# Another prologue order, score copies by ScalarE, and output turns in score slots, in an attention stage of a fused kernel

## The reference, cut to what matters

```
q, k = rope(x @ Wq, x @ Wk);  v = x @ Wv;  beta = x @ Wb + bb
p = softmax over j < i of (k_i . k_j) / 4          # strictly lower
A = p * beta + identity                             # lower triangular
u = solve_triangular(A, v)
o = softmax over j <= i of (q_i . k_j) / 4  applied to u;  out = o @ Wo
```

## Time and profile before

| | |
|---|---|
| time, median of 3 runs | 1138.64 us (1136.46 to 1138.84) |
| the profiled execution's own time | 1140.44 us |
| its span (first to last instruction) | 1138.5 us |
| busy: TensorE, weight loads | 742.7 us, 528.0 us |
| busy: VectorE, ScalarE, GpSimd | 562.3 us, 299.1 us, 238.5 us |
| mean granted TensorE clock | 0.799 |
| last instruction of the attention block | 505.98 us |
| inversions start (line 677) | 116.65, 207.61, 302.70, 395.14 us |

### The profile page before, as it was taken

One profiled execution on the slowest core, in us unless ns is written; L12 is line 12 of the kernel. 1 busy time (PEld: TensorE's weight loads), 2 busy tenths in 40 slices (PEclk: granted clock), 3 DMA queues, 4 the chain that ended last, 5 costly groups with the idle time before them and its releaser, 6 DMA issues. The chain is left out here.

```text
span 1138.5 us, 16783 instructions
## 1 busy us (share of the span) xinstructions
PE 742.7 (65%) x6078; PEld 528.0 (46%) x6079; DVE 562.3 (49%) x1556; ACT 299.1 (26%) x494; POOL 238.5 (21%) x251
## 2 busy tenths in 40 slices
PE   1967387777767757762054999998004550999980
PEld 1533264355445436442043999997001240566650
DVE  6796985885788582136300333333346551233322
ACT  1005144442542543311021344443002210211110
POOL 8003002111120210001775000004576005000005
PEclk9897689878979965666576999999556765899995
DMA  3691005122340901017934888886232002111113
GB/s 121 98 138 44 0 3 176 29 32 46 133 57 7 397 12 39 1 49 242 392 130 158 302 297 293 291 291 226 66 100 88 1 0 81 36 43 45 46 37 111
DMA packets 71264, 132.53 MB, mean 116 GB/s; under 512 B 11424, under 2 KB 35360, under 8 KB 70176
## 3 DMA queue, kind: packets, MB, share of 16 engines
q1 hardware_dynamic: 59168, 96.92, 28.9%
q0 software_dynamic: 7680, 20.98, 5.7%
q10 hardware_dynamic: 4352, 13.77, 3.2%
HBM read 77.18 MB, written 54.26 MB: 115 GB/s over the span
## 5 line engine op out<-in xcount | busy, mean ns | idle before, releaser
L1096 PE MATMUL scores<-wgu,zero 128*128 128x192 f32 x512 | 101.7, 345 | 2.7 <-DMA wd<-in_wd 2.7
L806 ACT ACTIVATE E<-scores 128x1280 f32<-128x1280 f32 x64 | 77.0, 1237 | 85.2 <-PE scores L354 54.0
L613 DVE TENSOR_REDUCE block_maxima<-scores 128x10 f32<-128x1280 f32 x64 | 92.3, 1486 | 12.5 <-PE scores L338 11.6
L1197 DVE TENSOR_TENSOR val<-sel,scores 128x192 f32<-128x192 f32 x64 | 22.7, 354 | 149.5 <-ACT sel L1239 149.5
L1253 POOL DMA_INDIRECT expert_rows<-xn_moe,scatter_slots x64 | 62.6, 977 | 133.2 <-DVE gather_slots L1173 114.0
L1096 PEld LDWEIGHTS scores<-wgu,zero 128*128 128x128 f32 x512 | 88.9, 204 | 3.2 <-DMA wd<-in_wd 3.1
L1580 PE MATMUL scores<-w,xgT 128*128 x184 | 88.8, 607 | 0.5 <-issue 0.5
L1089 PE MATMUL misc<-cf,xg 128*128 128x128 f32 x256 | 42.2, 290 | 65.2 <-DMA xg<-expert_rows 65.2
L1230 ACT COPY zero<-misc 128x512 f32<-128x512 f32 x64 | 37.5, 586 | 136.2 <-PE misc L1089 136.2
L911 POOL TENSOR_SCALAR_AFFINE_SELECT E<-E 128x256 f32<-128x256 f32 x64 | 27.0, 447 | 219.4 <-ACT E L806 219.3
L1113 PE MATMUL scores<-wd,slot 96*128 96x256 f32 x256 | 68.2, 391 | 0.5 <-ACT slot L1226 0.5
(11 more groups left out here) (232 smaller groups left out, 1526.1 us busy)
## 6 DMA issues: line engine op xcount, KB each, us to landing
expert_rows<-zero SPq DMA_DIRECT2D x32, 512.0 KB, 6.2
xg<-expert_rows SPq DMA_DIRECT2D x64, 256.0 KB, 3.4
expert_outputs<-xnT SPq DMA_DIRECT2D x64, 256.0 KB, 2.9
wgu<-in_wgu SPq DMA_DIRECT2D x32, 384.0 KB, 3.6
w<-in_w ACTq DMA_DIRECT2D x8, 1024.0 KB, 16.5
wd<-in_wd SPq DMA_DIRECT2D x32, 192.0 KB, 3.8
w<-in_w ACTq DMA_DIRECT2D x8, 512.0 KB, 19.0
split_heads<-E SPq DMA_DIRECT2D x8, 384.0 KB, 4.6
```

The lines of the kernel that those rows point to most:

```text
L613: nc.vector.tensor_reduce(bm[:, c, h, :], scores[:, slot, 0:WIDE].rearrange("p (a n) -> p a n", n=P), AX.X, ALU.max).then_inc(s_fd, 1)
L806: nc.scalar.activation(Eu(u)[:, h, :], scores[:, k % 2, 0:WIDE], ACT.Exp, scale=SCALE).then_inc(s_fa, 1)
L1096: ins = nc.tensor.matmul(scores[:, j % 2, t * 2 * F0:(t + 1) * 2 * F0], xgT[:, j % 2, k, t * P:(t + 1) * P], wgu[:, j // GE, j % GE, k, :] ...
```

## The change

What it does, part by part:

- **First rows.** The clears of the upper rows of unit 0's stacks go from GpSimd to VectorE's start. The rows of ones are filled as float pairs (`TWO_ONES`) over half as many elements. The clears of XT and XR both come after the normalization.
- **Heads by index first.** The columns of Wq and Wk are ordered so that a partition is dimension * 8 + head. A stack slot is then one contiguous piece of DRAM, 16 rows of 8 KB. The B stack is loaded in three copies (48, 32 and 16 rows) instead of six. ScalarE's queue issues the first k stack.
- **Projections 4 to 7** are made after row scores 3, 6, 9 and 12. ScalarE copies each into SBUF (`held`), and VectorE rotates them after the maxima of unit 0. Projection 3 and the beta columns change places.
- **First maxima.** The k maxima of unit 0 are turned before row score 10, and key score 0 comes before the turn of the q maxima.
- **Gather.** It collects in `turned` and no longer in `Y`; VectorE takes 12 of 16 copies instead of 8. Y's identity blocks are written in the prologue and in the solve of the unit before.
- **Sums** wait for the first transpose (`LB`) only, `join` for the second. The outputs of unit u-1 are divided after T1 steps 0 and 1 of unit u.
- **Output turns** go to the score slots 0 and 1, both after `attend(u, 1)`; the second half's copy goes to `bankD`.
- **Last unit.** Its q scores are made between the steps of its solve (`beside`), their exponentials go to the other half of E (`Eq`). Wo is loaded into `LB` after the last sums, not into E.

```diff
-PART_A = (0, 0, 1, 1, 0, 2)
-PART_B = (0, 1, 0, 1, 2, 0)
+RUNS_A = tuple((s, p, 1) for s, p in enumerate((0, 0, 0, 1, 1, 2)))
+RUNS_B = ((0, 0, 3), (3, 0, 2), (5, 0, 1))
...
+            def Eq(u):
+
+                return EE[:, u % 2] if u + 1 < UNITS else EE[:, (u + 1) % 2]
...
             def load_stack(q, u, c):
-                hg, b = unit(u)
-                x, order = {"k": (0, PART_A), "B": (0, PART_B), "q": (1, PART_A)}[c]
-                for s, part in enumerate(order):
-                    q.dma_start(stk[c][HD * s:HD * (s + 1), u % 2],
-                                scr[x, part, hg * P:(hg + 1) * P, b * T:(b + 1) * T]
-                                .rearrange("(h d) n -> d h n", d=HD)).then_inc((s_stq if c == "q" else s_stk)[u % 2], 16)
+                done = (s_stq if c == "q" else s_stk)[u % 2]
+                for s, part, n in RUNS_B if c == "B" else RUNS_A:
+                    to = stk[c][HD * s:HD * (s + n), u % 2].rearrange("p h n -> p (h n)")
+                    of = scr[int(c == "q"), u, part:part + n].rearrange("t (d h) n -> (t d) (h n)", h=GH)
+                    q.dma_start(to, of).then_inc(done, 16)
...
+            held = {4: EE[:, 0, 5, 0:2 * T], 5: EE[:, 0, 7, 0:2 * T], 6: AO_flat[:, 0:2 * T], 7: AO_flat[:, 2 * T:4 * T]}
...
-                    for w in range(5):
+                    for w in range(3):
                         project(w)
-                    pe.wait_ge(s_rf, 3)
+                    pe.wait_ge(s_rf, 1)
...
                     ins.then_inc(s_v, 1)
+                    project(3)
                     pe.wait_ge(s_vc, 1)
-                    project(5)
-                    pe.wait_ge(s_rf, 5)
-                    pe.wait_ge(s_ones, 1)
+                    pe.wait_ge(s_ones, 2)
...
+                    def beside(u, heads):
+
+                        if u + 1 < UNITS:
+                            key_scores(u + 1, heads)
+                        else:
+                            pe.wait_ge(s_ml[1], 48 * (u + 1))
+                            for h in heads:
+                                transposed_scores(u, 1, h)
...
                     def turn_outputs(u, hh):
                         pe.wait_ge(s_oc, 2 * u + hh + 1)
+                        pe.wait_ge(s_fa, use(1, u) + GH)
+                        of = bankD if hh else bankT
                         for it in range(NI):
-                            ins = nc.tensor.transpose(misc[:, hh, it * P:(it + 1) * P], bankT[:, it * P:(it + 1) * P], identf)
+                            ins = nc.tensor.transpose(scores[:, hh, it * P:(it + 1) * P], of[:, it * P:(it + 1) * P], identf)
...
+                        if m == 10:
+                            turn_maxima(0, 0)
+                            pe.wait_ge(s_mr, 1)
                         row_scores(0, m, m % 2)
-                    turn_maxima(0, 0)
+                        if m in (3, 6, 9, 12):
+                            project(m // 3 + 3)
+                    key_scores(0, [0])
                     turn_maxima(0, 1)
                     pe.wait_ge(s_mr, 2)
-                    key_scores(0, [0, 1])
-                    project(6)
-                    key_scores(0, [2, 3, 4])
-                    project(7)
-                    key_scores(0, [5, 6, 7])
+                    key_scores(0, range(1, GH))
...
-                        pe.wait_ge(s_y, 2 * (u + 1))
-                        if u:
-                            pe.wait_ge(s_fa, use(1, u - 1) + GH)
-                            pe.wait_ge(s_ao, 2 * u)
-                        else:
+                        pe.wait_ge(s_y, 2 * u + 1)
+                        if u == 0:
                             pe.wait_ge(s_vc, 1 + NT)
...
+                    for c in ("B", "k", "q"):
+                        ins = nc.vector.memset(upper_rows(c, 0), 0.0)
+                    ins.then_inc(s_z0, 1)
...
-                        for s in range(2, P // SB):
+                        for s in range(1, P // SB):
...
-                        link(nc.vector.transpose(LB[:].rearrange("p j i -> p i j"), Y[:]))
-                        link(nc.vector.memset(Y[:], 0.0))
-                        nc.vector.memset(flat[:, 0:SB * SB - 1].rearrange("p (a b) -> p a b", b=SB + 1)[:, :, 0], 1.0)
-                        link(nc.vector.memset(flat[:, SB * SB - 1:SB * SB], 1.0))
+                        link(nc.vector.transpose(LB[:].rearrange("p j i -> p i j"), turned[:]))
...
                     for m in range(16):
                         maxima(0, m, m % 2)
...
-                    for w in range(5, 8):
+                    for w in range(4, 8):
                         rotate_and_split(w)
...
                             scaled_sums(u, q)
+                            if u and q < 2:
+                                outputs(u - 1, q)
...
+                    act.wait_ge(s_pw[0], 16)
+                    load_stack(act, 0, "k")
...
+                    def hold(w):
+                        act.wait_ge(s_pj, w + 1)
+                        nc.scalar.copy(held[w], misc[:].rearrange("p b n -> p (b n)")).then_inc(s_rf, 1)
+
+                    hold(4)
+                    hold(5)
                     rows(0, 0)
+                    hold(6)
+                    hold(7)
                     rows(0, 1)
...
+                    for c in ("B", "k", "q"):
+                        zero_rows(c, 1)
+                    one_rows(1)
+                    pool.wait_ge(s_z0, 1)
+                    one_rows(0)
                     link(nc.gpsimd.memset(zero[:], 0.0))
                     nc.gpsimd.sem_inc(s_ones, 1)
-                    link(nc.gpsimd.memset(XT[:], 0.0))
-                    nc.gpsimd.sem_inc(s_z, 1)
                     pool.wait_ge(s_xn, NT)
                     link(nc.gpsimd.memset(XR, 0.0))
+                    nc.gpsimd.sem_inc(s_z, 1)
+                    link(nc.gpsimd.memset(XT[:], 0.0))
                     nc.gpsimd.sem_inc(s_z, 1)
...
                     sp.wait_ge(s_pw[0], 16)
-                    load_stack(sp, 0, "k")
+                    load_stack(sp, 0, "B")
                     store_parts(sp, 1)
-                    load_stack(sp, 0, "B")
```

More of the change, by code:

```diff
@@ L323, in turn_maxima @@
                         pe.wait_ge(s_nms, 2 * u + c + 1)
-                        pe.wait_ge(s_fd, 16 * u + (9 if u and not c else 16))
+                        pe.wait_ge(s_fd, 16 * u + (16 if c else 9))
                         nc.tensor.transpose(scores[0:96, c, WIDE:WIDE + 64].bitcast(BF16),
@@ L445, in solve @@
                                 ins.then_inc(s_s, 1)
-                                if not last:
-                                    key_scores(u + 1, [2 * it + 1])
+                                beside(u, [2 * it + 1])
                                 pe.wait_ge(s_sn, 3 * u + it)
@@ L460, in solve @@
                             ins.then_inc(s_us, 1)
-                            if not last:
-                                if it < NI - 1:
-                                    key_scores(u + 1, [2 * it + 2] if it else [0, 1, 2])
-                                else:
-                                    denominators(u + 1)
+                            if it < NI - 1:
+                                beside(u, [2 * it + 2] if it else [0, 1, 2])
+                            elif not last:
+                                denominators(u + 1)
                             pe.wait_ge(s_un, 4 * u + it + 1)
@@ L538, in _ @@
                                 for m in maxima_due(q):
+                                    if u and m < 2:
+                                        pe.wait_ge(s_ao, 2 * u - 1 + m)
                                     if m >= 2:
@@ L549, in _ @@
                         solve(u)
+                        if last:
+                            pe.wait_ge(s_uv, 4 * (u + 1))
+                            attend(u, 0)
+                            attend(u, 1)
+                            turn_outputs(u, 0)
+                            turn_outputs(u, 1)
+                            break
                         pe.wait_ge(s_ml[1], 48 * (u + 1))
                         transposed_scores(u, 1, 0)
-                        if not last:
-                            turn_denominators(u + 1)
-                            turn_g(u + 1)
-                            pe.wait_ge(s_g, u + 2)
+                        turn_denominators(u + 1)
+                        turn_g(u + 1)
+                        pe.wait_ge(s_g, u + 2)
                         pe.wait_ge(s_uv, 4 * (u + 1))
@@ L602, in rotate_and_split @@
                         nc.vector.sem_inc(s_parts, 1)
-                    for w in range(5):
+                    identity_blocks()
+                    for w in range(4):
                         rotate_and_split(w)
-                    dve.wait_ge(s_vc, 1)
-                    bcol = VB[:, :, D:D + H]
-                    link(nc.vector.tensor_tensor(bcol, bcol, bb[:].unsqueeze(1).to_broadcast([P, NT, H]), ALU.add))
```

(11 more changed lines are left out.)

112 lines of the change are left out of this document (63 added, 49 removed).

## The result

The changed kernel took 1106.83 us, the median of 4 runs (1105.47 to 1107.94), against 1138.74 for the kernel before, measured beside it: a ratio of 0.9721, 95% interval 0.9700 to 0.9742. The profiled execution took 1105.99, span 1104.1, mean granted clock 0.811. Forecast was 1103.5.

A forecast was written before the change was run, and what follows sets the result against it. The first block was taken as a sequence of stages, read by each stage's last wait. Gains 8.0 + 4.2 + 8.1 + 16.2 = 36.5 from 1140.4 gave 1103.9, stated as 1103.5; range 1093 to 1119.

The forecast's parts named there:

- Prologue: Start to first inversion: its first multiplication comes at 108.7 instead of 116.65, gain 8.0, bounds −2 and 12.5.
- the rotations would have lost 7: Rotations 4 to 7 beside GpSimd's selects: 0.5 charged, bounds 0 and 7; the skill's two-SBUF-input rule would make it 7.
- Stacks: Prologue: k and B stack loads land at 45.6, before VectorE arrives at 46.0; at 109 GB/s 48.7, costing 2.7.
- Rival 3: Stack copies get worse, contiguous sources reaching few engines; whole gain eaten, or time near 1187; chance 0.03.
- Between units: Three times, gather to inversion 1.4 each, 4.2; earlier T1 and later output divisions in units 1 to 3, 8.1.
- Last unit: q scores between the solve's steps, at the clock of unit 0: last division at 475.4 against 491.61, gain 16.2.
- Rival 1: The last solve stays at 1.2 GHz: 14 less gain, 1118; chance 0.15.
- My first paragraph: Change touches only the first of four blocks, ending near 506; what is saved there moves everything behind one for one.
- some 2: Last step of the sum: 1103.9 is some 2 less if measured as the median was; forecast stated as 1103.5.

The follow-up runs named there:

- e4: Changed kernel with the last unit's eight q scores and exponentials behind the solve again; ratio 0.9756 to the kernel before, on the slower chip.
- e5: e4 with the same score matmuls also issued between the solve's steps, read by nobody; 1110.91 us against 1140.27 for the kernel before, ratio 0.9741.
- e7: Changed kernel with nine filler float matmuls, read by nobody, at the start of blocks 2 and 4; 1107.10 us, ratio 0.9723 to the kernel before.
- e1: Changed kernel with GpSimd's clears in the old order and number, XT cleared before the normalization; ratio 0.9772 to the kernel before.
- e2: Changed kernel with the gather split 8 and 8 again and identity blocks set behind its transpose; block ended 7.5 us later than the changed kernel's, no total given.
- e3: Changed kernel with the first sums waiting for both transposes of an inversion; block ended 6.7 us later than the changed kernel's, no total given.
- e9: Changed kernel with five filler float matmuls, read by nobody, at the start of blocks 2 and 4; 1101.33 us, ratio 0.9672 to the kernel before.

## Why the prediction was right

- **Prologue: 8.0 forecast, 9.2 measured.** The normalization ended at 15.8 (15.2 forecast): the three VectorE clears end at 7.8, behind X's arrival, and cost 1.4, not 0.2. The first projection started at 18.51 (18.0), the first rotation at 22.32 (23.6). This last gain is luck as far as these runs show: with the same code up to there the rotation started at 22.3 in four profiles and at 24.1 to 24.5 in three (e4, e5, e7), where the multiplication came at 108.5 to 109.4. Projection 3 took 6.44 at the low clock (6.1). The maxima ran from 44.76 to 80.06 (46.0 to 81.85) with stalls of 2.60, 2.50, 1.49 and 2.49 (four of 2.5). The four rotations behind them took 19.4 and not 18.6, 0.8 more (0.5). The inversion started at 107.49 (108.7).
- **GpSimd against VectorE.** With GpSimd idle all eight instructions took 0.41, and e1 brought 3.75 back. The Trainium skill (SBUF — State Buffer, "Who interferes with whom") lets one of the two block the other for a whole instruction in this case; the runs agree. Its other rule is that a VectorE instruction with two SBUF inputs contends with a GpSimd instruction that reads SBUF. Here it cost VectorE little: most of these steps took 0.77 to 0.89 instead of 0.69. GpSimd paid more: its selects took 0.57 to 0.88 each, where those of the kernel before took 0.40 while VectorE was idle (90.0 to 91.9). By the rule as I priced it the rotations would have lost 7; the measurement says 0.8.
- **Stacks.** They landed at 43.0 (45.6 forecast). From 36 to 40 us the queue moved 129 to 131 GB/s, as before. From 26 to 62 us, stores included, it moved 5.15 MB in 2374 packets at a mean of 143 GB/s; the kernel before moved 5.65 MB in 6040 packets at 138 (34 to 75 us). So eight times longer rows hardly raised the rate. The Trainium skill's rule that a copy reaches only the ports of its partitions (SBUF — State Buffer, "Door 1: The DMA port swizzle") fits that; the rate measured lies above its 109 GB/s, and no run took the new layout away by itself. Rival 3 didn't occur.
- **Between units: 4.2 and 8.1 forecast.** From the gather to the multiplication 1.5 each (1.4), T1 and outputs 2.65 each (2.7). Both terms have the size forecast, but 1.5 was lost again in the solves and 1.0 in the last sums stage. From the first to the last inversion 10.7 were gained, 2.4 of them because the kernel before had a low-clock stretch in its unit 1. e2 gave its term back; e3 gave back 1.2 of the 2.65 per unit; the other 1.5 (the later place of the outputs, as I take it) was not tried alone. In both the sums stages were longer on top, 1.1 to 2.5 each, and I had no term for that.
- **Last unit: 16.2 forecast, 16.7 measured** from the last T1 to the last division, which ended at 453.3 (near 455). Its parts hold too: the first copy of U came 3.7 later behind the last T1 (3.8 forecast), from the first to the last copy it took 14.9 (15.2), and behind that 7.0 instead of 22.7 (7.2). e4 and e5 split it: 9.5 is the moved work and 2.5 the clock in the solve and behind it. Of the 4.8 between e4's outputs and those of the kernel before, 2.1 is the new place of the output turns and 2.1 the clock. The forecast had no term for the output turns; it took them for neutral. Rival 1's price, the whole unit at 1.2 GHz with the scores in the solve, was not tried.
- **Not in the sum.** 3.5 more from the last division to the end of the block, at 1.00 where it had been 0.50, and 7.4 given back in later blocks. My first paragraph says that what is saved in the attention block "moves everything behind it forward one for one". That step failed: 41.8 were saved in it and 34.4 arrived. The two gates with their transposes lost 6.6 of that, and e9, which only raises the clock there, got 5.5 back. The sum came out near by luck: two errors of 5.3 and 7.4 nearly cancelled. Its last step is also loose: 1103.9 less "some 2" is 1101.9 and not 1103.5, and the profiled run of the changed kernel was not slower than the median.
- **Not tried.** The stacks' new layout, the late output turns and the identity blocks were never taken back by themselves on one chip with the changed kernel. The shares of all experiments are read from one profile each; their totals are not.

## What to carry to other kernels

In this kernel TensorE had stretches at half clock in many stages that VectorE paced, and they moved when anything ahead of them moved. So before a difference of 2 to 3 us is put down to an edit, look in every profile at the granted clock of the few stages where TensorE is the limit. Where TensorE idles ahead of a short stage that it bounds, fill the idle time and no more with matmuls that nobody reads, and count them by their measured length: five gained 5.5 us, nine gained nothing. And weigh what GpSimd's memsets do to VectorE: beside the normalization they cost 10.1 (e1), while three of these clears, moved to VectorE itself, cost 1.4.

## What the runs showed of the hardware

- With identical instructions ahead of it, the pair of first projections took 7.13 (changed kernel, e2, e3, e9) or 8.90 to 9.35 (e4, e5, e7), and the first rotation started at 22.3 or at 24.1 to 24.5: a spread of 2 us in the profile that no edit made. The profile's granted clock is 1.00 from 18 us on in both cases, so it doesn't tell them apart.
- GpSimd's selects and VectorE's steps with two SBUF inputs slow each other: 0.57 to 0.88 instead of 0.40 for a select beside an idle VectorE, 0.77 to 0.89 instead of 0.69 for a step.
- The clock can stay at 0.50 through a busy stage: the gate's 32 matmuls ran back to back for 7.09 at 0.50, directly behind 16 transposes.
- The kernel before took 1171.55 on the chip of e1 to e4 and 1138.74 to 1140.27 beside the other runs, a difference of 2.9%. The attention block is alike: the first multiplication came at 106.4 to 108.5 in e2 to e4, and at 107.5 to 109.4 in the changed kernel, e5, e7 and e9. What lies behind that block is longer, 666 in e1 against 640 in the changed kernel.
